# A two-layer attention and feed-forward kernel on one core: part of the key and value weight splitting moved to GpSimd, the inverse roots moved into the first pair, the last phase ahead of it reordered

## What is computed

```python
xn = layernorm(x)
x = x + attention16heads(xn, Wq, bq, Wk, bk, Wv, bv, Wo, bo) + quantised_linear(xn, w_int8, w_scale, bias)
xn = layernorm(x)
x = x + compare_attention(xn, left, right) + token_mix_ffn(xn, W_r, W_k, W_v, mu_r, mu_k)
# attention16heads: rotate q and k, scores / 8, causal mask, softmax, times v, times Wo
# quantised_linear: x scaled by the largest |xn| of the whole input, rounded to int8
```

## Time and profile before

| | |
|---|---|
| median of three runs | 1081.67 us |
| the profiled execution | 1081.11 us |
| its span | 1079.3 us |
| TensorE matmul busy | 1019.6 us (94%) |
| VectorE busy | 869.1 us (81%) |
| ScalarE busy | 715.4 us (66%) |
| GpSimd busy | 764.1 us (71%) |
| scores of pair 0 begin | 46.25 us |
| scores of pair 2 begin (last of ring 0 on TensorE done) | 76.14 us |

### The profile page before, as it was taken

The page is one execution under the profiler, slowest core; times in us unless marked ns, Lnnn a source line. Parts: engine busy times, 40 slices in busy tenths (PEclk is TensorE's granted clock), DMA queues, the critical chain, the costliest instruction groups (busy, mean ns, idle before and its releaser), DMA issues.

```text
span 1079.3 us, 24087 instructions
## 1 busy us (share of the span) xinstructions
PE 1019.6 (94%) x8446; PEld 705.6 (65%) x8446; DVE 869.1 (81%) x1824; ACT 715.4 (66%) x1950; POOL 764.1 (71%) x936
## 2 busy tenths in 40 slices
PE   5779999999999999999999999999999987799998
PEld 4446665666667666666666666666667764577666
DVE  7988889778778788777777777777777758999995
ACT  5958886666666667666666666666666736667774
POOL 3666667777768787867677878777777554668884
PEclk9999999999999999999999999999999998989999
DMA  9523434333432323332333323333322000000001
GB/s 299 184 89 109 148 127 142 92 117 105 121 102 89 109 89 94 97 116 89 96 101 108 89 90 94 117 95 99 107 89 89 2 1 1 21 20 21 30 31 40
DMA packets 99703, 98.73 MB, mean 91 GB/s; under 512 B 13312, under 2 KB 95360, under 8 KB 98944
## 3 DMA queue, kind: packets, MB, share of 16 engines
q1 hardware_dynamic: 99584, 97.19, 29.0%
HBM read 56.25 MB, written 40.90 MB: 90 GB/s over the span
## 4 chain that ended last, share of the span: by engine, by line
PE 69%; DVE 18%; ACT 5%; issue 4%; POOL 3%; DMA 1%; DVEq 0%; SPq 0%; ACTq 0%; POOLq 0%
PE bank L1595 20%; PE bank L1679 12%; PE bank L1693 12%; PE bank L1710 7%; PE bank L1666 6%; PE bank L1667 5%; PE bank L1668 2%; DVE arena L1470 2%; PE bank L1883 2%; PE bank L1829 2%; ACT arena L829 1%; DVE nm L1440 1%; POOL arena L615 1%; DVE nm L1312 1%; DVE x_sb L1492 1%
## 5 line engine op out<-in xcount | busy, mean ns | idle before, releaser
L615 POOL TENSOR_SCALAR arena<-arena,rc 128x128 f32<-128x128 f32 (+3 forms) x512 | 275.1, 555 | 205.1 <-DVE rc L1320 202.8
L829 ACT ACTIVATE arena<-bank,nm 128x256 f32<-128x256 f32 (+3 forms) x512 | 268.1, 526 | 81.9 <-DVE nm L1312 72.3
L1312 DVE TENSOR_REDUCE nm<-bank 128x1 f32<-128x256 f32 (+3 forms) x512 | 230.4, 480 | 90.1 <-PE bank L1668 86.9
L1679 PE MATMUL bank<-ident,arena 128*128 128x128 f32 x1280 | 217.4, 278 | 11.9 <-DVE arena L1327 6.5
L1679 PEld LDWEIGHTS bank<-ident,arena 128*128 128x128 f32 x1280 | 145.0, 142 | 49.2 <-DVE arena L1327 23.8
L837 ACT ACTIVATE arena<-bank 128x512 f32<-128x512 f32 (+3 forms) x256 | 111.3, 435 | 80.0 <-PE bank L1679 79.7
L1667 PE MATMUL bank<-arena 128*128 128x256 f16 (+3 forms) x512 | 153.7, 300 | 0.0
L1666 PE MATMUL bank<-arena 128*128 128x256 f16 (+3 forms) x512 | 147.8, 301 | 5.1 <-ACT arena L829 3.4
L1693 PE MATMUL bank<-arena 128*64 128x512 f32 (+3 forms) x1024 | 151.9, 439 | 0.0
L1327 DVE COPY arena<-bank 128x512 f32<-128x512 f32 (+3 forms) x256 | 124.1, 485 | 22.6 <-PE bank L1679 18.5
L1693 PEld LDWEIGHTS bank<-arena 128*64 128x64 f32 x1024 | 67.8, 136 | 94.3 <-issue 73.6
(11 more groups left out here) (171 smaller groups left out, 2295.3 us busy)
## 6 DMA issues: line engine op xcount, KB each, us to landing
arena<-scr SPq DMA_DIRECT2D x320, 128.0 KB, 2.7
scr<-arena SPq DMA_DIRECT2D x256, 128.0 KB
arena<-in_weights SPq DMA_DIRECT2D x5, 1024.0 KB, 7.3
x_sb<-in_x SPq DMA_DIRECT2D x8, 512.0 KB, 8.8
out<-x_sb SPq DMA_DIRECT2D x16, 256.0 KB, 2.1
xscr<-arena SPq DMA_DIRECT2D x12, 256.0 KB, 2.9
xsh<-xscr SPq DMA_DIRECT2D x6, 256.0 KB, 3.4
xsl<-xscr SPq DMA_DIRECT2D x6, 256.0 KB, 3.6
```

Of the source, the lines that this page charges most:

```text
L615: last = pool.tensor_scalar(pr[slot][:, OFF[i]:OFF[i + 1]], pr[slot][:, OFF[i]:OFF[i + 1]], rc[:, slot, i:i + 1], 1.0, ALU.mult, ALU.mult)
L829: act.activation(pr[slot][:, OFF[i]:OFF[i + 1]], s_tile[i], ACT.Exp, bias=nm[:, slot, i:i + 1], accum_out=sm[:, slot, i:i + 1]).then_inc(e ...
L1312: dve.tensor_reduce(nm[:, slot, i:i + 1], s_tile[i], AX.X, ALU.max, negate=True).then_inc(max_done, 1)
L1679: last = pe.transpose(banks[5 + h][:, (i - j) * P:(i - j + 1) * P], pr[2 * par + h][:, OFF[i] + j * P:OFF[i] + (j + 1) * P], ident[:])
```

## The change

- GpSimd makes the low parts of the first two key pieces: it scales the staged weights in place (L585 of the changed kernel), waits for itself, and subtracts the high part (L587). VectorE makes the low parts of the other two key pieces right behind those of Wq, ahead of the first `even_terms`. Phase 1's even half waits for GpSimd's pieces (`key_lo`), its odd half for VectorE's.
- GpSimd makes the bf16 copy of the int8 weights in its `ring(-2)` and the high part of Wv in `ring(-1)`, each ahead of `rotate`. ScalarE loses both.
- The statistics of batch 7 go from ScalarE's `later_weights(-2)` to VectorE's `second_gap(-1)`.
- The inverse roots go from `ring_end(-1)` to `second_gap(0)`. All four tiles of `normal_rows(1)` go to the end of ScalarE's `ring(0)`. `row_maximum(1)` goes from the first gap to the second. The maxima over Wo's four parts, two in ring 0 and one each in rings 1 and 2, become one each in rings 1 and 2 and two in ring 3.
- In VectorE's `ring(-1)`, `even_terms(4)` and Wv's low part go behind the maxima of pair 0's second head.
- The first `fill` has 24 matmuls in place of 60.

```diff
+            for i, (src, (high, low)) in enumerate(halves(G_K)):
+                if i < 2:
+                    pool.wait_ge(qk_hi, 4 + i + 1)
+                    pool.tensor_scalar(src, src, inv[:, G_K:G_K + 1], 1.0, ALU.mult, ALU.mult).then_inc(key_scaled, 1)
+                    pool.wait_ge(key_scaled, i + 1)
+                    pool.tensor_tensor(low, src, high, ALU.subtract).then_inc(key_lo, 1)
...
                 normalise(n, 1, n % 2)
+                if n == 3 - AHEAD:
+                    pool.wait_ge(c_loaded, 16 * 3)
+                    pool.tensor_copy(w8[:], w8st.rearrange("p (k c w) -> p k c w", k=KT, w=2)[:, :, :, 0]).then_inc(w8_done, 1)
+                elif n == 4 - AHEAD:
+                    pool.wait_ge(setup_done, 2)
+                    pool.tensor_scalar(wh[:, C_V:C_O], wst_v, inv[:, G_V:G_V + 1], 1.0, ALU.mult, ALU.mult).then_inc(wv_hi, 1)
                 rotate(n + AHEAD - 1)
...
-                elif n == 3 - AHEAD:
-                    row_sums(7)
-                    act.wait_ge(c_loaded, 16 * 3)
-                    act.activation(w8[:], w8st.rearrange("p (k c w) -> p k c w", k=KT, w=2)[:, :, :, 0], ACT.Copy).then_inc(w8_done, 1)
-                    act.wait_ge(setup_done, 2)
-                    weights_high(G_V, wv_hi)
...
-                if 0 <= n < NB - 1:
+                if 1 <= n < NB - 1:
                     normal_rows(n + 1, (0,))
...
-                    normal_rows(n + 1, (2, 3))
+                    normal_rows(n + 1, (2, 3) if n else range(NT))
...
             pairs_low(G_Q, 1)
+            pairs_low(G_K, 1)
...
-                elif n == -AHEAD:
-                    pairs_low(G_K, 0)
-                    pairs_low(G_K, 1)
...
-                if 0 <= n < NB:
+                if 0 <= n < NB and n != 1:
                     row_maximum(n)
...
                 if n == -1:
-                    weights_low(G_V, (wv_hi, 1), wv_lo)
+                    dve.wait_ge(x_loaded[NB - 1], 16)
+                    statistics((NB - 1) * NT, 3)
                 elif n == 0:
-                    part_maximum(0)
-                    part_maximum(1)
-                elif n == 1 or n == 2:
-                    part_maximum(n + 1)
+                    dve.wait_ge(act_stats, NB - 4)
+                    inverse_roots(slice(1, NB), 1)
+                elif 1 <= n <= 3:
+                    if n == 1:
+                        row_maximum(1)
+                    part_maximum(n - 1)
+                    if n == 3:
+                        part_maximum(3)
...
-                if n == -1:
-                    dve.wait_ge(act_stats, NB - 3)
-                    inverse_roots(slice(1, NB), 1)
-                elif n == 7:
+                if n == 7:
...
+                if n == -1:
+                    weights_low(G_V, (wv_hi, 1), wv_lo)
+                    inverse(n + 1, 1, e)
+                    even_terms(n + AHEAD)
                 pt_whole(n, 3)
                 odd_terms(n + AHEAD)
...
-                if f < 2:
-                    pe.wait_ge(qk_lo, 2 * f + e + 1)
+                if f == 0:
+                    pe.wait_ge(qk_lo, e + 1)
+                elif f == 1:
+                    pe.wait_ge(*((qk_lo, 3) if e else (key_lo, 2)))
...
-            FILL = (0, 60, 0, 50)
+            FILL = (0, 24, 0, 50)
```

More of the change, by code:

```diff
@@ L231, in build @@
         act_stats = sem("act_stats")
+        key_scaled = sem("key_scaled")
+        key_lo = sem("key_lo")
         xn1_done = sem("xn1_done")
@@ L1374, in row_statistics @@
                 dve.wait_ge(x1_done, 2 * b + 2)
-                statistics(b * NT, b + 3)
+                statistics(b * NT, b + 4)
             def ring(n):
@@ L1392, in ring @@
                 second_gap(n)
-                even_terms(n + AHEAD)
+                if n != -1:
+                    even_terms(n + AHEAD)
                 inverse(n + 1, 0, e)
@@ L1400, in ring @@
                 maxima(n + 1, 1, e, (3,))
+                if n == -1:
+                    weights_low(G_V, (wv_hi, 1), wv_lo)
+                    inverse(n + 1, 1, e)
+                    even_terms(n + AHEAD)
                 pt_whole(n, 3)
                 odd_terms(n + AHEAD)
-                inverse(n + 1, 1, e)
+                if n != -1:
+                    inverse(n + 1, 1, e)
                 ring_end(n)
```

## The result

The changed kernel takes 1087.62 us, median of 4 runs (1085.89 to 1088.55); the kernel before, run beside it, takes 1081.26 (1080.43 to 1084.47, 4 runs). The ratio of their means is 1.0051, 95% interval 1.0027 to 1.0076, so 5.5 us slower, between 2.9 and 8.2. The forecast was 1084.7, in a range from 1079.5 to 1089.0, as "no change", which ends at 5.4 us. The result lies inside the range and on that edge. The profiled execution took 1087.97 us and its span is 1086.2, against 1081.11 and 1079.3 before. So 6.9 us have to be found between the two profiles.

What follows compares the result with a forecast made beforehand. VectorE was taken to pace the lead-in, with TensorE 94% busy over the span. Terms 0.9 - 3.8 + 2.5 + 2.2 + 1.5 = +3.3 us on 1081.1 gave 1084.4; with 0.6 for the median, forecast 1084.7, range 1079.5 to 1089.0.

Steps and rivals of the forecast that it cites:

- The keys' low pieces: Before the first scores: VectorE and GpSimd take turns on the pieces, delaying phase 1 and the keys' DMA; +0.9 us.
- Ring -1: First maximum to ring 0: 13.3 us against 17.1, with Wv's high part taking 3.0 on GpSimd; -3.8 us.
- Ring 0: First maximum to third transpose block's copy: roots 3.5 us and a wait of 1.05 added, maxima and waits removed; +2.5 us.
- the clock: TensorE's granted clock falls after two idle times, before v(0) and before phase 5's odd half; 1.1 us each, +2.2 us.
- the second fall of the clock: After TensorE idles while the roots run in ring 0, phase 5's odd half and av(0) run slower; 1.1 us.
- Rings 1 to 3: Two Wo maxima lengthen ring 3 by 1.2 us, row_maximum(1) in a tighter gap costs ring 1 0.3; +1.5 us.
- The rival in which TensorE's clock stays up: In the lead-in, all as forecast but without the 2.2 us for falls of TensorE's clock: 1082.5 us; chance 0.22.
- The rival with queueing gone: GpSimd's new instructions leave VectorE's pieces alone, Wv's high part takes 2.0 us, no clock falls: 1080.6 us; chance 0.14.
- The rival of dear forms on GpSimd: GpSimd becomes the bound: Wv's high part 5.0 us, scalings and int32 copy dearer, +3.1 us: 1087.8 us; chance 0.15.
- the signs of being wrong: Wq's pieces ending at 23 us, pair 2's scores before 75, or a difference arising after 115 us, where nothing is changed.

Runs made afterwards that it cites:

- filled run: Changed kernel plus 62 unused TensorE matmuls ahead of v(0) and 54 ahead of pair 0's last transpose, filling both idle times: 1083.53 us, ratio 1.0002 to the kernel before.
- the same filling: 62 unused TensorE matmuls ahead of v(0): in the changed kernel 1.0017; in the changed kernel with keys undone and roots back, 1082.15 us, 0.9991.
- the run with the roots in the gap: Changed kernel with the keys' part undone and the inverse roots in ring -1's second gap, behind batch 7's statistics: 1082.22 us, ratio 0.9991 to the kernel before.

## Why the prediction was right, and where its terms were off

From the first scale to ring 4 the forecast was +3.3 us, and the profile has 101.52 us against 97.41, +4.1. The main mechanism was found where the forecast put it: time won ahead of ring 0, and more than that lost inside it, to the roots and to TensorE's clock, and in rings 1 and 3. Two steps of the keys' term failed, and the other terms were off in size. Part of the agreement is luck: the first two terms came out 1.8 us lower than forecast and the others 2.6 higher. Ring 0's first maximum at 61.27, forecast "near 61.2", is luck as well, because a start that was 1.8 us late made up for those two terms. And the forecast's own sum is 1081.1 + 3.3 + 0.6 = 1085.0; it was written down as 1084.7.

1. **The keys' low pieces, forecast +0.9, measured -0.3.** The turn-taking is as told: the pieces end 9.8 us behind the scale, forecast 10.1, and a piece that meets a subtraction is held for its length. VectorE reaches Wv's maximum 17.05 us behind the scale, before 16.64: +0.4. Two steps failed. The first scores were to come 1.35 us later with the keys' transfers; they start 28.72 us behind the scale, before 28.68. The transfers had slack: in the queue's own timeline the loads' issues begin 0.9 us later behind the scale than before, but the last two took 2.06 us before and 0.90 now. And VectorE was to be free at 47.9: I counted the small scaling (0.94 with GpSimd beside it) as fixed, and it fell to 0.23.
2. **Ring -1, forecast -3.8, measured -4.4.** The term that failed is Wv's high part on GpSimd: 2.01 us, where I took 3.0 between my ends of 2.0 and 3.4. It also started 0.1 us ahead of the first maximum and not 0.8, because it waits for the scale that VectorE makes right before, so only 0.4 us of that 1.0 reached VectorE. The lower end, the slope of 0.86 ns a column from the earlier trace rows, was the price to the hundredth. VectorE's wait behind it is 2.48 us, forecast 2.9. The Trainium skill's figure ("GPSIMD Engine Reference", section 3.1) gives an estimate of 3.1 us; the measurement decides.
3. **Ring 0 and 4. the clock, forecast +4.7 together, measured +6.5.** Before, the second maximum of ring 0, the first term behind the roots' new place and ring 1's first maximum read

```profile
65.61 0.74 DVE L1312 TENSOR_REDUCE nm<-bank 128x1 f32<-128x128 f32 x2
...
70.09 0.75 DVE L1290 SCALAR_TENSOR_TENSOR arena<-bank,bcol,cosk 128x512 f32<-128x512 f32 x1 [0.40 <-PE bank L1595]
...
76.63 0.42 DVE L1312 TENSOR_REDUCE nm<-bank 128x1 f32<-128x256 f32 x1 [1.19 <-PE bank L1668]
```

To the second maximum it is now 66.11 - 61.27 = 4.84 us against 65.61 - 64.16 = 1.45: +3.4, forecast 1.05 for the wait and 1.1 for the clock. This is the step that failed most. The filled run says how it splits: with full clock the wait is 1.14 us, the forecast's 1.05, and the low clock adds 2.2 and not 1.1, because transposes and scores behind v(0) are slow as well. From there to the end of the roots 6.16 us against 4.48: +1.7, forecast 3.5 - 1.2 - 0.8 = 1.5; the roots take 3.50 us as forecast. From the roots to ring 1, 7.93 us against 6.54: +1.4, forecast 1.1 for the second fall of the clock: phase 5's odd half takes 0.63 us a matmul, where full clock has 0.38.
5. **Rings 1 to 3, forecast +1.5, measured +2.3.** Ring 3 is 1.20 longer, as forecast. Ring 1 was to cost 0.3 and costs 1.13: the moved maximum (1.21 us at 85.93) had been nearly free in the first gap, where VectorE waits for TensorE (1.23 us at 82.53), and costs nearly all of its length in the second. The run with it moved back shows it.

The rival in which TensorE's clock stays up is what the fillings make: +0.2 us by the ratio, between -1.1 and +1.5, where the forecast has +0.8 (1082.5). The rival with queueing gone would have needed VectorE's pieces at 23 us. The rival of dear forms on GpSimd fell, too: they were cheap (0.85 a scaling, 0.66 the copy, 2.01 the values' weights), although the time came out where that rival stood (1087.8): the same number for another reason. The chances were off in one respect: 0.17 for slower by over 5.4 us left the clock at 1.1 us a fall with 1.2 more at the upper end, and the falls measured 1.5 to 2.2 and 0 to 2.7. One of the signs of being wrong came about, a difference that arises after 115 us (the 1.0 us in the second layer); it is as small as what executions differ by there.

What stays open: the steps taken back one by one give 2.5 to 4 us each by the ratios, more than their stretches in the profiles, and the changed kernel's own ratio comes from four runs. The 1.0039 against all later runs of the kernel before would fit them better; that is a reading, not a result. A kernel with both fillings, row 1's maximum in the first gap and the part maxima in rings 0 to 2 was not run.

## What to carry to other kernels

A step moved off the engine that sets the pace is paid again where it lands if the next engine's work is queued behind it there. Here 5.9 us of roots in front of ring 0 became 3.5 us inside it, plus two idle times of TensorE with low clock behind them. With both filled the kernel was level with the one before (1.0002), and the one with the roots left in place was no slower than that (0.9988). Price an idle time of TensorE by all that runs behind it until the clock is back, and only if somebody waits for that: the same filling took 1.9 us off ring 0 in one order of the work and nothing in the other. A gap's slack is a property of that gap, so a maximum that was nearly free in one gap can cost nearly its full length in the next.

## What the runs showed of the hardware that was not expected

- A VectorE instruction over 8 columns takes 0.23 us alone and 0.94 beside a GpSimd sum, one over 28 columns 0.19 and, above, 1.08 twice in a row. Each of these long ones ends 0.03 to 0.04 us behind the GpSimd instruction that it meets (the run with the roots in the gap: 54.54 and 55.66 us against 54.50 and 55.62), whatever its own size.
- GpSimd pays, too: its scaling of 512 columns takes 0.86 us beside VectorE's pieces and 0.69 without them, the subtraction 1.20 and 1.16.
- GpSimd's scaling of 2048 columns from f32 to f16 takes 2.01 us, 0.98 ns a column, while 512 columns cost 0.69 us or more.
- The moment at which the first weights land differs between executions although their transfer is issued at the same 1.77 us: the scale is ready at 19.1 to 20.3 us in eight profiles with the keys' part and at 17.6 to 20.0 in five without, a spread of up to half the effect measured here.
